# Attention gives up a PSUM bank to the feed-forward layers, and the places of all steps are set anew

## What is computed

```python
def ffn(x):                       # weights ternary, 256 -> 1024 -> 1024 -> 1024 -> 256
    h = silu(x @ w1.T * s1) * (x @ w2.T * s2)
    h = gelu(h @ h1.T * t1)
    h = gelu(h @ h2.T * t2)
    return h @ w3.T * s3
def attention(x):                 # 16 heads of 16; each row sees 24 rows at fixed offsets back
    q, k, v = split(x @ Wqkv + bqkv)
    scores = q . k[i - offset] * 0.25 + pos_bias
    out = sum(softmax(scores) * v[i - offset])
    return out * sigmoid(x @ Wgate + bgate) @ Wout + bout
x = x + 0.5 * ffn(norm(x)); x = x + attention(norm(x)); x = x + 0.5 * ffn(norm(x))
```

## Time and profile before

| what | us |
|---|---|
| median of 3 runs | 1532.85 |
| their range | 1529.48 to 1532.97 |
| the profiled execution | 1529.28 |
| its span, first to last instruction | 1527.4 |
| TensorE busy | 1472.4 |
| VectorE / ScalarE / GpSimd busy | 1025.6 / 679.3 / 572.1 |

### The profile page before, as it was taken

How to read it: one execution, slowest core, us unless ns; L and a number is a source line. 1 busy time by engine, 2 the same in 40 slices (tenths; PEclk the granted TensorE clock), 3 DMA queues, 4 the chain that set the end, 5 groups by cost and what they waited for, 6 DMA issues and landing times.

```text
span 1527.4 us, 19080 instructions
## 1 busy us (share of the span) xinstructions
PE 1472.4 (96%) x6914; PEld 1207.8 (79%) x6914; DVE 1025.6 (67%) x1349; ACT 679.3 (44%) x1063; POOL 572.1 (37%) x466
## 2 busy tenths in 40 slices
PE   6989999999999999999899999899999999989998
PEld 5777878787877788878687878788888878778887
DVE  6524777875867677859684978596577777872322
ACT  7653545343535344444353534435344444343532
POOL 3011263462462436251735170807225345353100
PEclk9999999999999999999999999999999999999999
DMA  8765668766575775858656777585675867854332
GB/s 297 274 244 172 208 215 319 245 236 214 193 258 180 253 275 188 279 173 288 234 182 209 264 243 249 186 288 177 218 251 179 287 226 235 285 194 145 103 118 71
DMA packets 189347, 338.21 MB, mean 221 GB/s; under 512 B 15680, under 2 KB 138688, under 8 KB 188864
## 3 DMA queue, kind: packets, MB, share of 16 engines
q1 hardware_dynamic: 189248, 336.93, 64.4%
HBM read 314.85 MB, written 30.41 MB: 226 GB/s over the span
## 4 chain that ended last, share of the span: by engine, by line
PE 83%; POOL 5%; DVE 4%; DMA 3%; ACT 3%; issue 2%; SPq 0%; DVEq 0%; POOLq 0%; ACTq 0%
PE f_bank L1155 27%; PE f_bank L1156 27%; PE a_banks L1230 7%; PE f_bank L1115 6%; PE f_bank L1116 6%; PE f_bank L1184 3%; PE f_bank L1185 3%; PE a_banks L1250 2%; POOL acc L773 2%; DMA weights_hi<-in_ffn_w 2%; DVE slot L1026 1%; DMA slot<-keys_and_values 1%; POOL h_lo L787 1%; PE f_bank L1103 1%; DVE slot L1070 1%
## 5 line engine op out<-in xcount | busy, mean ns | idle before, releaser
L1155 PE MATMUL f_bank<-h_hi,wring 128*128 128x512 f32 x2048 | 810.9, 396 | 8.0 <-DMA wring<-weights_hi 3.8
L1156 PE MATMUL f_bank<-h_lo,wring 128*128 128x512 f32 x2048 | 799.6, 390 | 0.0
L1155 PEld LDWEIGHTS f_bank<-h_hi,wring 128*128 128x128 f32 x2048 | 385.6, 188 | 92.1 <-DVE h_lo L926 4.7
L1156 PEld LDWEIGHTS f_bank<-h_lo,wring 128*128 128x128 f32 x2048 | 385.8, 188 | 80.9 <-issue 2.2
L856 ACT ACTIVATE h_hi<-f_bank,colv 128x512 fp32r<-128x512 f32 x256 | 176.4, 689 | 544.5 <-PE f_bank L1156 544.2
L926 DVE TENSOR_TENSOR h_lo<-f_bank,h_hi 128x512 fp32r<-128x512 f32 x256 | 175.8, 687 | 250.2 <-ACT f_bank L857 249.1
L787 POOL TENSOR_TENSOR h_lo<-f_gated,h_hi 128x512 fp32r<-128x512 f32 x128 | 170.3, 1343 | 348.0 <-ACT h_hi L850 347.5
L1115 PE MATMUL f_bank<-fT_hi,w_in 128*128 128x512 f32 x512 | 205.8, 402 | 9.2 <-ACT f_gated L845 3.8
L1116 PE MATMUL f_bank<-fT_lo,w_in 128*128 128x512 f32 x512 | 200.9, 392 | 0.0
L1026 DVE TENSOR_TENSOR slot<-slot,a_banks 128x1280 f32<-128x1280 f32 (+4 forms) x124 | 170.6, 1376 | 16.3 <-DMA slot<-keys_and_values 16.2
L1032 DVE TENSOR_REDUCE S<-slot 128x80 f32<-128x1280 f32 (+4 forms) x124 | 171.7, 1385 | 4.3
(11 more groups left out here) (115 smaller groups left out, 1141.4 us busy)
## 6 DMA issues: line engine op xcount, KB each, us to landing
wring<-weights_hi SPq DMA_DIRECT2D x248, 512.0 KB, 4.8
slot<-keys_and_values SPq DMA_DIRECT2D x128, 384.0 KB, 4.6
slot<-keys_and_values SPq DMA_DIRECT2D x64, 640.0 KB, 4.3
slot<-keys_and_values SPq DMA_DIRECT2D x312, 128.0 KB, 4.5
slot<-keys_and_values SPq DMA_DIRECT2D x64, 256.0 KB, 5.6
weights_hi<-in_ffn_w SPq DMA_DIRECT2D x16, 512.0 KB, 6.8
keys_and_values<-kv_out SPq DMA_DIRECT2D x32, 256.0 KB, 3.2
slot<-in_ffn_w SPq DMA_DIRECT2D x10, 512.0 KB, 5.3
```

What stands on the lines that cost most here:

```text
L1155: pe.matmul(bank[:, :], hi, h_hi[src][:, k, :], start=(k == 0), stop=False)
L1156: last = pe.matmul(bank[:, :], hi, h_lo[src][:, k, :], start=False, stop=(not general and k == KH - 1))
```

## The change

It does four things. `q_bank` now holds the softmax weights of the first block too: they are written once the scores have used the queries. So the next sub-tile's query projection waits for this sub-tile's row sums and for the weighing of its first block, where it waited for the scores. The bank that comes free, the second half of `a_banks1`, becomes the fifth of the feed-forward banks, from the end of the opening on; rows show it as `a_banks1`. The first block's exponential no longer waits for the previous residual. And `TIMES`, `FOLLOW`, `OPENING` and `STARTS` have new numbers, which moves steps on every engine. Line numbers behind the opening shift by one to five.

```diff
--- before.py
+++ after.py
@@ -29,14 +29,14 @@
 
 STEPS = ["stats", "turn", "kv0", "q", "kv1", "gate", "score", "score step", "ahead", "max", "weigh", "weigh step",
          "z", "out"]
-TIMES = [3.65, 9.56, 11.46, 12.91, 17.19, 25.44, 22.37, 3.94, 7.13, 53.75, 61.23, 3.2, 93.09, 4.73]
-
-FOLLOW = dict(silu=-1.5, gate=-0.08, cut=1.63, low=1.99, gelu=-0.77,
-              lo=1.12, residual=-0.87, store=2.93, fill=23.53, stats=-0.47, turn=4)
-
-OPENING = dict(block=9.27, block_step=1.86, compare=2.04, turn=8.2, input=13.0, count=52.85)
-STARTS = [50.0, 118.7, 184.3, 274.4, 343.7, 411.3, 489.6, 575.0,
-          642.8, 722.6, 789.0, 867.0, 962.9, 1038.6, 1110.1, 1179.0]
+TIMES = [3.68, 9.15, 11.23, 13.34, 17.43, 25.38, 22.36, 3.96, 7.42, 53.74, 61.23, 3.2, 93.17, 4.79]
+
+FOLLOW = dict(silu=-1.74, gate=-0.11, cut=1.62, low=1.84, gelu=-0.32,
+              lo=1.34, residual=-0.58, store=3.64, fill=30.91, stats=-0.48, turn=4)
+
+OPENING = dict(block=9.28, block_step=1.85, compare=1.82, turn=8.13, input=13.0, count=52.41)
+STARTS = [50.0, 118.7, 184.4, 273.7, 338.5, 411.3, 489.3, 575.0,
+          640.4, 722.6, 787.9, 863.5, 962.9, 1038.4, 1107.7, 1178.9]
 
 
 class Counts:
@@ -155,10 +155,6 @@
     def qk_done(a, u, g):
         return per_group.at(a, groups_of[a.c].index((u, g)) + 1)
 
-    def qk_before(a):
-
-        return per_group.at(a, 0)
-
     def acc_done(a, u, g):
 
         return per_acc.at(a, (acc_ops[a.c][0] if u else 0) + max(g, 1))
@@ -246,9 +242,11 @@
         fb = [ctx.enter_context(nc.psum_tensor(f"f_bank{i}", [P, 512], fp32)) for i in range(4)]
         pairs = [ctx.enter_context(nc.psum_tensor(f"a_banks{i}", [P, WBLK], fp32)) for i in range(2)]
 
-        t_bank, q_bank, *p_banks = [pair[:, n * 512:(n + 1) * 512] for pair in pairs for n in range(2)]
+
+        t_bank, q_bank, p_bank, fifth = [pair[:, n * 512:(n + 1) * 512] for pair in pairs for n in range(2)]
+        fb.append(fifth)
         q = q_bank[:, :].rearrange("p (n d) -> p n d", n=SB)
-        probs = [b[:, 0:HEADS * NU].rearrange("p (h e) -> p h e", h=HEADS) for b in p_banks]
+        probs = [b[:, 0:HEADS * NU].rearrange("p (h e) -> p h e", h=HEADS) for b in (q_bank, p_bank)]
 
         def w12(m, w, k):
             o = ((m % 2) * 4 + w * 2 + k) * P
@@ -500,13 +498,15 @@
             return (name, r.j, *rest)
 
 
-        uses = []
-        for name, (r, *rest) in [*pe_steps(opening()), *pe_steps(timeline()[0])]:
-            uses += [key(name, r, *rest, w) for w in range(2)] if name == "f_in" else [key(name, r, *rest)]
-        use_of = {use: i for i, use in enumerate(uses)}
+        bank_of, used_before, last_use = {}, {}, {}
+        for steps, banks in (opening(), 4), (timeline()[0], 5):
+            for name, (r, *rest) in pe_steps(steps):
+                for use in [key(name, r, *rest, w) for w in range(2)] if name == "f_in" else [key(name, r, *rest)]:
+                    bank = len(bank_of) % banks
+                    bank_of[use], used_before[use], last_use[bank] = bank, last_use.get(bank), use
 
         def f_bank(name, r, *rest):
-            return fb[use_of[key(name, r, *rest)] % 4]
+            return fb[bank_of[key(name, r, *rest)]]
 
         def counted(name, j, *rest, attempt):
 
@@ -867,13 +867,15 @@
 
             def a_exp_(a):
                 act.wait_ge(a_less, a.at(1, 1))
-                after(act, a_x, a.at(1, 0))
                 for n in range(SB):
+                    if n == 1:
+
+                        after(act, a_x, a.at(1, 0))
                     act.activation(probs[n], S[:, n, :, :], ACT.Exp).then_inc(a_exp, 1)
 
             def a_zT_(a):
                 act.wait_ge(a_zturned, a.at(1, 1))
-                act.activation(zT[:, :, :].rearrange("p k n -> p (k n)"), p_banks[0][:, :], ACT.Copy).then_inc(a_zT, 1)
+                act.activation(zT[:, :, :].rearrange("p k n -> p (k n)"), p_bank[:, :], ACT.Copy).then_inc(a_zT, 1)
 
             schedule({"w_cut": w_cut, "f_scale": f_scale, "f_evict": f_evict, "f_silu": f_silu_, "f_cut": f_cut,
                       "f_gelu": f_gelu_}, opening())
@@ -1078,7 +1080,7 @@
             def a_residual(a):
                 dve.wait_ge(a_bout, a.at(1, 1))
                 dve.wait_ge(a_wo, a.at(1, 1))
-                dve.tensor_tensor(xa[:, a.u, :, :], p_banks[0][:, :].rearrange("p (n d) -> p n d", n=SB), xa[:, a.u, :, :],
+                dve.tensor_tensor(xa[:, a.u, :, :], p_bank[:, :].rearrange("p (n d) -> p n d", n=SB), xa[:, a.u, :, :],
                                   ALU.add).then_inc(a_x, 1)
 
             schedule({"w_scale": w_scale, "w_max": w_max, "w_merge": w_merge, "f_stats": f_stats_, "f_tlo": f_tlo_, "f_gate": f_gate, "f_lo": f_lo_,
@@ -1090,9 +1092,8 @@
         def _(pe):
             def bank_free(attempt, *use):
 
-                i = use_of[use] - 4
-                if i >= 0:
-                    pe.wait_ge(*emptied(*uses[i], attempt=attempt))
+                if used_before[use]:
+                    pe.wait_ge(*emptied(*used_before[use], attempt=attempt))
 
             def f_turn(r, bp, attempt):
                 bank = f_bank("f_turn", r, bp)
@@ -1217,7 +1218,11 @@
                 if what == "kv0":
                     pe.wait_ge(a_xT, a.at(1, 1))
                 elif what == "q":
-                    after(pe, a_qk, qk_before(a))
+                    if a.i:
+
+                        before = subs[a.i - 1]
+                        pe.wait_ge(a_sum, before.at(1, 1))
+                        pe.wait_ge(a_pv, per_group.at(before, sum(n == 0 for n, g in groups_of[before.c])))
                 else:
                     pe.wait_ge(a_kv, a.at(SB, 2 if what == "gate" else 1))
 
@@ -1237,7 +1242,7 @@
 
                 for kc in range(KD):
                     for n in range(SB):
-                        last = pe.transpose(p_banks[0][:, kc * ST + n * P:kc * ST + (n + 1) * P],
+                        last = pe.transpose(p_bank[:, kc * ST + n * P:kc * ST + (n + 1) * P],
                                             z[:, n, kc * P:(kc + 1) * P], ident[:, :])
                 last.then_inc(a_zturned, 1)
 
@@ -1247,7 +1252,7 @@
                 pe.wait_ge(a_zT, a.at(1, 1))
                 for n in range(SB):
                     for e in range(2):
-                        last = pe.matmul(p_banks[0][:, n * D:(n + 1) * D], zT[:, e, n * P:(n + 1) * P], wo[:, e, :],
+                        last = pe.matmul(p_bank[:, n * D:(n + 1) * D], zT[:, e, n * P:(n + 1) * P], wo[:, e, :],
                                          start=(e == 0), stop=(e == 1))
                 last.then_inc(a_wo, 1)
```

## The result

The changed kernel is faster by about 0.6%.

What follows compares the result with a forecast made beforehand. TensorE, busy 1472.4 of 1527.4 us, was taken as the bound, so only its waits could be won. Terms summed to -15.3 us, less 3.3 given back: -12, from a median of 1532.85 to 1520.8 us, range 1512 to 1533.

Steps and rivals of the forecast that it cites:

- restarts: TensorE's slow first matmul after each wait, 0.50 instead of 0.39 us, goes with twelve waits: -1.3 us.
- give-back: Time other engines' moved steps, not followed in detail on VectorE and SP, return to TensorE's waits: 3.3 us taken.
- seam: First hidden step behind the opening reuses the preceding step's bank: +1.7 us, hidden by a later DMA wait, cost 0.
- Part 1: Fifth feed-forward bank: bank waits after 100 us, 8.0 us in ten, shrink to 2.0; with pass 5's, 6.8 us saved.
- Nothing: ScalarE's two extra table loads, 2.6 us, cost nothing as long as five banks cover them.
- Part 2: Shared query bank: the next query projection never waits for it, smallest slack 7.3 us before, about 6 after; cost 0.
- part 3: Behind the opening, a bank stall of 1.7 us near 61 us, covered by a weight-block wait at 92.34; cost 0.
- Part 4: New step places: `aT` waits -4.3, a8 -3.1 and its clock -1.7, a5 -2.1, a11 +1.3, a14 +1.8, `z` +0.9 us.
- rival (a): Half the gain comes back because waits on GpSimd's chains do not shrink: about -6 us, 1527; chance 0.20.
- Rival (b): No change, 1532: new 3.5 us waits at three more moved turns, each with a clock fall; chance 0.14.
- (c): Slower, 1538: earlier weight fills in SP's queue delay key and value loads, net +5 us; chance 0.09 together with (d).
- (d): The query projection's wait for the shared bank bites, needing 6 us more delay than seen; chance 0.09 together with (c).

Runs made afterwards that it cites:

- second profile of the changed kernel: The changed kernel measured once more, unaltered, beside the version with six moved steps; 1518.13 us, ratio 0.9925 to the kernel before.
- a10 repaired: Changed kernel with a10's norm step (`a_rstd`) moved ahead of an addition of a9 in GpSimd's queue; 1522.36 us, ratio 0.9936 to the kernel before.

## Why the prediction came out as it did

The side and the range were right, and the median came within 0.4 us of the number. That closeness is luck: the gain was 8.9 us rather than 12, the median of before came out lower by about as much, and within the sum too small and too large terms offset each other. By its own terms, from the two profiles:

| term | forecast | measured |
|---|---|---|
| bank waits behind 100 us | -6.8 | -4.3 (8.0 to 3.7) |
| `aT` at a0, a4, a9, a11, a14 | -4.3 | -4.1 (a14 keeps 0.25) |
| a8, turn and copy | -3.1 | -3.1 |
| clock at a8 | -1.7 | -1.7 |
| a5 | -2.1 | -0.8 (1.61 left) |
| a11, turn | +1.3 | +2.1 (4.30) |
| a14, turn | +1.8 | +1.5 |
| a15, turn, and `h_lo` at 499.50 | none | -0.6 + 0.4 |
| `z` and `zT` | +0.9 | -0.4 (4.83 to 4.45) |
| restarts: busy time less what the clock cost | -1.3 | -3.1 (1465.6 to 1462.5) |
| give-back: a10 | in the 3.3 | +0.9 turn, +1.7 `aT`, +2.9 clock |
| give-back: clock at a11 | in the 3.3 | +0.6 (1.7 to 2.3) |
| seam, bank and DMA waits, 60 to 100 us | 0 | -0.7 (1.06 + 0.33 + 2.70 to 2.06 + 1.37) |
| sum | -12 | -8.7, as the span |

**Part 1** had the right mechanism. The wait of 1.82 us at pass 5 went. The step that failed is "Left of them is 2.0"; 3.7 is left. The size was off mainly because I took the waits of before and made them shorter, and did not look for new ones. In the new order a score of a sub-tile stands ahead of two gate products on VectorE, and three waits at `f_out` (L1185), 0.84, 0.44 and 0.91 us, were not there before. For the second of them VectorE has

```profile
766.85 1.49 DVE L1034 TENSOR_REDUCE S<-slot 128x80 f32<-128x1280 f32 x1
768.25 1.40 DVE L937 SCALAR_TENSOR_TENSOR f_gated<-f_bank,colv,f_gated 128x512 f32<-128x512 f32 x2
```

With the new places and four banks the same three places wait 1.24, 1.33 and 1.74 us, so they come from the order, and the fifth bank only shortens them. But the shortening was too good as well: with the old places, where only one new wait of 0.31 us appears, 3.2 are left. There the waits of 1.10 and 1.71 us came down to 0.74 and 1.10, by less than the 0.91 of one use. Why was not traced.

The table loads are 19 for SiLU and 27 for GELU as read from the order, 1283 ns each. "Nothing" for them holds over the program, but not at a10, where a load and a GELU pair stand between two of TensorE's steps. The Trainium skill (ScalarE: Activation LUTs, "What ACT_TABLE_LOAD costs") adds a drain to the load. Here the load at 884.31 starts 0.02 us behind the end of the `a_hat` row, and the GELU at 885.60 0.01 us behind the end of the load, so these rows show no drain.

**Part 2** and **part 3** came out as forecast: no wait for the softmax weights, and a stall of 2.06 us (1.7 forecast) with a shorter DMA wait behind it.

**Part 4** was right at a8, a14 and the five `aT` waits that it moved; of the five that it left, a10's grew. It was too good for the two turns that wait for GpSimd. At a5 the wait is 0.66 us with the new places and four banks, and 1.61 with five. At a11 it is 3.46 and 4.30. GpSimd's queue did not get faster when TensorE did, which was the argument for rival (a). That the rival did not come true is a matter of size: 3.2 us given back, against 9 for "half". Rival (b) wanted three new waits of some 3.5 us at moved turns, each with a fall of the clock. One came, a14's, of 1.53 us and without a fall.

**The miss** is a10. I followed the turns that moved ahead of feed-forward steps, and took a10's copy at the 0.69 us that it has in the earlier trace rows. The give-back of 3.3 us stood for such places, and a10 and a11's clock alone were 6.1 us.

The restarts made up for part of that, and here the step that failed is the price of one, "(0.50 instead of 0.39)". TensorE's busy time, less what was lost to the clock, fell by 3.1 us. Twelve waits are gone, as forecast, but each takes more with it than its slow first matmul. A matmul in a stream starts 0.23 us behind the one ahead (four from 303.50 to 304.41) and has a row of 0.39, so ahead of a wait the last 0.16 us have no other matmul beside them and count as busy. With the 0.11 of the forecast that is 0.27 a wait and 3.2 in all, an estimate that meets the 3.1 measured. The other profiles agree in the main: less the clock's cost the busy time is 1461.3 to 1462.5 us in the nine with five banks, which have 22 to 27 waits between 75 and 1450 us, and 1465.2 to 1465.6 in the three with four banks, which have 33 to 36.

**Slower** needed (c) or (d). Undoing the fills changed nothing, and nothing waited for the queries' bank, so neither came true here.

## What to carry to other kernels

A buffer more for one engine is worth what its waits cost in the new order, not in the old one. What the engine wins can be partly given back at results of engines that did not become faster: here 3.2 of 8.8 us in the new order, and nothing in sum in the old one. And a wait costs more than its bracket, here by some 0.27 us. So after such a change, read the waits again by place, and repair queues one place at a time: each repair showed the next one (a10, then `z` of a9, then `z` of a10), and six moved steps of GpSimd and VectorE brought nearly as much as the change itself (0.9864 beside 0.9925, and that beside 1).

When a wait of an engine goes and the time stays, look at the next two steps behind it before doubting the wait.

## What the hardware showed beyond what was expected

- The clock's falls, all to 1.2 GHz, were not equally long. Behind nearly the same waits (1.21 and 2.41 us at a10, 4.3 at a11) TensorE lost 2.9 and 2.3 us in one execution and 1.7 and 1.7 in another. In all, the second profile of the changed kernel lost 6.8 us to the clock and that of the run with the old fills 10.1, though the two wait alike but for 1.1 us for a weight block and 0.7 us for `z`. So two profiles of one order can differ by some 3 us with hardly a difference in waits, a third of what was to be measured here.
- The fall behind the seam stall (clock 0.61 from 64 to 68 us in the first profile) went with the stall, and yet pass 1 starts no earlier without them (94.67 us) than in the second profile of the changed kernel, which has both (94.53).
- Behind a wait of 1.91 us for `z` of a7 the clock fell in the profile with a10 repaired. It did not fall there in the seven other profiles with this wait, in which it is 1.99 us (at 751.67 in the changed kernel) and 1.41 to 1.92. Which waits make it fall is not settled by these runs.
